# A six-stage fp32 network on one core: the state-space stage reordered, and constant TensorE products put into waits

## The chip, the core and the metric

One NeuronCore of a Trainium2 chip runs the whole program in one launch. The metric is the device time of that launch in microseconds (us). TensorE (PE) multiplies, VectorE (DVE), ScalarE (ACT) and GpSimd (POOL) do the elementwise work, and SyncE's queue (SP) issues most of the transfers.

## What is computed

2048 tokens of width 128 pass through six blocks with residual connections, all in fp32. Cut to what matters here:

```python
x = x + 0.5 * ffn(layernorm(x))     # F, run 0: two layers of local attention (8 heads, window 64) and gated MLP
x = x + ssm(layernorm(x))           # S
x = x + 0.5 * ffn(layernorm(x))     # F, run 1: the same weights
x = x + 0.5 * moe(layernorm(x))     # M, moe 0: 8 experts, the best 2 of each token
x = x + unit(layernorm(x))          # U: gated unit (its Toeplitz part acts on a sequence of length 1)
x = x + 0.5 * moe(layernorm(x))     # M, moe 1

def ssm(x):                         # state size N = 64 for each of the 128 channels
    u = layernorm(x) * gamma + beta             # so x is normalised twice in a row
    h[t] = exp(-exp(log_A) * dt) * h[t-1] + B * dt * u[t]
    y[t] = sum_n C[n] * h[t, n] + D * u[t]
    return y @ W_out.T + b_out
```

## The kernel before, in words

X lies in SBUF as 128 channels (partitions) by 2048 tokens, worked on in four chunks c of 512 tokens. Every engine has its own hand-written program and runs it strictly in order; engines meet at semaphores. So the order written down for each engine is the schedule, and a wait at the head of one engine's program holds all that stands behind it.

**The state-space stage** (plan letter S; line numbers are those of the profile). Each chunk is normalised twice; p = 0 and p = 1 name the two passes. One pass is: `ssm_centred(c, p)` on PE (L526, a product with the centring matrix into bank `SN_CEN[c]`), `ssm_square` on ACT (L1154), `ssm_variance` on PE (L532, a product with the averaging matrix into bank `SN_VAR`), `ssm_root` on ACT (L1163 Ln, L1166 Exp), `ssm_normed` on DVE (L1599 for p = 0, L1602 and L1604 for p = 1). The order of the eight passes is the list `SN_ORDER`; squares, logs and roots have two buffers, used in turn. Then `ssm_transpose(c)` (PE, L540) turns the chunk into 64-token blocks, and `ssm_input(c)` copies the halves out on ACT (L1170) and DVE (L1608). When all four chunks are there, PE forms the block states: 128 products of 64x64 weights with 31 columns (L924, 256 matmul instructions), in four groups of 32, one PSUM bank each. Behind each group DVE runs two scans over the blocks (L1912). Meanwhile ACT takes eight exponentials over the output decays (`decays_exp`, L1183) and POOL multiplies each by C·B (L2172, counted by `gt_done`). PE then forms the outputs in four groups (L936, 256 instructions, each group waits for two more scans; before the first, all eight `gt_done`), transposes them (L945), multiplies by W_out (L956), and DVE adds into X (L1926). `base(c)` (DVE, L1888) adds the bias and the once-normalised value into X; only L1926 needs it. `state_decays(1, .)` (ACT, L1177) are two exponentials that L924 needs.

The stage's first passes are woven into the end of F, run 0, where the last MLP chunk (L777 to L790, `mlp_output(7)`) and the last residual (`mlp_residual`, DVE L1788 and L1793, which counts `x_ffn`) run.

**F, run 1** begins with the first norm (L549, L553, DVE L1627), then steps s of attention: two projections (L602), square sums on PE (L659), scores (L634), and so on.

**M** sends token rows to DRAM by expert: PE writes token rows and router scores of a chunk (`token_rows` L576, `route` L570, `rank` L584 and L585), DVE picks the experts (L1654 to L1708), ACT scales the rows (L1213 to L1225), POOL issues eight indirect transfers for each chunk (L2114). DVE then computes the tile map in 24 chained steps (`map_dve`), SP loads the first tiles, and PE runs 39 tiles of 128 rows: a transpose (`take`, L976), the hidden product (L984), the output product (L994). The outputs go to DRAM by POOL (L2121), come back by SP, and `combine` (L1019) adds the two experts of each token; DVE adds them to X (L1931). **U** weaves its norm (L1031, L1037), up products (L1050), ACT's silu (L1514), gates (DVE L2033), down products (L1057) and the routing of moe 1 into one order; `enter(c)` is token_rows and route of a chunk once its `x_unit` is done.

## Time and profile before

| | us |
|---|---|
| median of 3 runs (lowest, highest) | 1125.36 (1124.89, 1128.22) |
| profiled execution, its own time | 1124.78 |
| its span in the trace | 1123.0 |
| PE busy (share of the span) | 978.7 (87%) |
| DVE, ACT, POOL busy | 733.0, 686.3, 524.6 |

The span counts from the first to the last instruction of the trace; the execution's own time is 1.8 us longer. TensorE's clock has two levels, and the profile lists the level granted in each stretch as a share of full speed: 1.00 is 2.4 GHz, 0.50 is 1.2 GHz. Its mean over the span is 0.942.
### The profile page before, as it was taken

What the parts mean: (1) busy time and instruction counts of PE and PEld (TensorE: products, weight loads), DVE (VectorE), ACT (ScalarE), POOL (GpSimd) and SP (SyncE); (2) the same over time, 40 slices, a digit from 0 to 9 for tenths busy, and PEclk for the clock granted to TensorE, in tenths of its full rate; (3) what the DMA queues carried; (4) which work ended last, traced back from release to release, by engine and by line L of the source; (5) the groups of instructions that cost most, each with busy time, mean ns of one, the idle gap of its engine ahead of it and who ended that gap; (6) DMA issues with size and microseconds to landing.
All of it is one profiled execution on the core that took longest, in us unless ns stands there. A gap on an engine that the chain in (4) does not pass through costs nothing.

```text
span 1123.0 us, 26079 instructions
## 1 busy us (share of the span) xinstructions
PE 978.7 (87%) x9072; PEld 628.4 (56%) x9072; DVE 733.0 (65%) x1689; ACT 686.3 (61%) x1329; POOL 524.6 (47%) x392
## 2 busy tenths in 40 slices
PE   4889999999998968789999999999828996856995
PEld 1445555555555347255555555556428994435995
DVE  1678787787877554378777877778674442665442
ACT  3577686686684572577776776684615663834661
POOL 2555466566442515455444544552463550263552
PEclk9899999999999987899999999999968998877998
DMA  5656464364444600355444444443331222012224
GB/s 180 165 152 144 114 162 115 86 143 114 93 98 104 78 1 3 91 118 115 111 99 97 114 105 98 103 110 82 133 112 53 69 75 82 19 49 66 68 68 127
DMA packets 89712, 109.99 MB, mean 98 GB/s; under 512 B 20368, under 2 KB 74384, under 8 KB 88816
## 3 DMA queue, kind: packets, MB, share of 16 engines
q1 hardware_dynamic: 82160, 91.17, 34.2%
q0 software_dynamic: 4544, 9.35, 2.4%
q10 hardware_dynamic: 2880, 7.81, 2.2%
q8 instruction: 75, 1.23, 0.5%
q14 instruction: 53, 0.43, 0.1%
HBM read 62.66 MB, written 12.07 MB: 67 GB/s over the span
## 4 chain that ended last, share of the span: by engine, by line
PE 74%; ACT 8%; DVE 7%; issue 4%; DMA 4%; POOL 1%; SPq 1%; ACTq 0%; DVEq 0%; POOLq 0%
PE banks L602 9%; PE banks L984 7%; PE banks L994 7%; PE banks L690 5%; PE banks L676 5%; PE banks L651 4%; PE banks L634 4%; PE banks L683 4%; PE banks L790 3%; PE banks L746 3%; PE banks L735 3%; PE banks L659 2%; PE banks L610 2%; DMA arena<-arena 2%; PE banks L1019 2%
## 5 line engine op out<-in xcount | busy, mean ns | idle before, releaser
L2142 POOL TENSOR_TENSOR arena<-arena 128x1024 f32<-128x1024 f32 x64 | 150.9, 2357 | 308.6 <-DVE arena L1735 302.4
L2131 POOL TENSOR_TENSOR arena<-arena 128x1024 f32<-128x1024 f32 x64 | 150.8, 2357 | 27.1 <-ACT arena L1244 27.1
L602 PE MATMUL banks<-arena 128*128 128x512 f32 x256 | 138.8, 630 | 7.1 <-DVE arena L1627 5.9
L1236 ACT ACTIVATE arena<-banks,arena 128x512 f32<-128x512 f32 x128 | 80.7, 682 | 102.0 <-PE banks L683 101.5
L2121 POOL DMA_INDIRECT moe_outs<-arena x78 | 80.9, 1037 | 96.2 <-DVE arena L1986 88.6
L1470 ACT ACTIVATE arena<-banks,arena 128x128 f32<-128x128 f32 x312 | 89.0, 369 | 56.3 <-PE banks L984 56.3
L1727 DVE TENSOR_REDUCE arena<-banks 128x4 f32<-128x512 f32 x128 | 82.4, 685 | 56.7 <-PE banks L634 56.6
L2114 POOL DMA_INDIRECT moe_rows<-arena x64 | 63.7, 996 | 87.0 <-DVE arena L1708 66.7
L1735 DVE TENSOR_TENSOR arena<-arena 128x1024 f32<-128x1024 f32 x64 | 77.9, 1218 | 23.4 <-DMA arena<-arena 23.4
L994 PE MATMUL banks<-arena 128*128 x624 | 86.4, 281 | 3.3 <-ACT arena L1470 2.8
L984 PE MATMUL banks<-arena 128*128 128x128 f32 x624 | 86.8, 284 | 0.3 <-issue 0.2
L1244 ACT ACTIVATE arena<-banks,arena 128x512 f32<-128x512 f32 x128 | 80.7, 688 | 7.6 <-DMA arena<-arena 7.2
L1741 DVE TENSOR_TENSOR arena<-banks,arena 128x512 f32<-128x512 f32 x128 | 81.8, 680 | 0.0
L683 PEld LDWEIGHTS banks<-arena 128*128 128x128 f32 x512 | 59.5, 140 | 39.7 <-issue 32.3
L994 PEld LDWEIGHTS banks<-arena 128*128 128x128 f32 x624 | 76.6, 193 | 7.5 <-issue 6.4
L984 PEld LDWEIGHTS banks<-arena 128*128 128x128 f32 x624 | 79.2, 199 | 1.4 <-issue 0.9
L651 PE MATMUL banks<-arena 128*64 128x65 f32 x2048 | 74.8, 225 | 3.6 <-ACT arena L1236 1.4
L1249 ACT ACTIVATE arena<-banks 128x1024 f32<-128x1024 f32 x64 | 65.6, 1025 | 19.8 <-PE banks L602 18.1
L651 PEld LDWEIGHTS banks<-arena 128*64 128x64 f32 x2048 | 65.7, 137 | 17.9 <-issue 17.9
L683 PE MATMUL banks<-arena 128*128 128x128 f32 x512 | 67.2, 272 | 4.7 <-DVE arena L1741 4.7
L602 PEld LDWEIGHTS banks<-arena 128*128 128x128 f32 x256 | 46.1, 201 | 45.0 <-issue 36.6
L634 PE MATMUL banks<-arena 64*64 64x128 f32 x2048 | 67.7, 270 | 1.5 <-DVE arena L1721 1.5
(230 smaller groups left out, 1944.3 us busy)
## 6 DMA issues: line engine op xcount, KB each, us to landing
arena<-arena SPq DMA_DIRECT2D x256, 128.0 KB, 3.7
arena<-rstd SPq DMA_DIRECT2D x128, 256.0 KB, 4.3
arena<-moe_rows SPq DMA_DIRECT2D x78, 64.5 KB
arena<-in_mw SPq DMA_DIRECT2D x2, 2048.0 KB
arena<-moe_outs SPq DMA_DIRECT2D x16, 256.0 KB, 4.9
arena<-in_rot ACTq DMA_DIRECT2D x12, 256.0 KB, 3.3
arena<-in_wa ACTq DMA_DIRECT2D x2, 1026.0 KB, 6.7
arena<-ssm_a SPq DMA_DIRECT2D x4, 512.0 KB, 6.2
```

Source lines behind the costliest of these rows:

```text
L602: mm(bank[k], w_qkv[d][:, w0:w0 + P], (YA, YM)[d][:, c * C:(c + 1) * C], start=True, stop=True).then_inc(proj, 1)
L634: last = mm(bank[3 + e][r0:r0 + WIN, c0:c0 + P].rearrange("p (b n) -> p b n", b=2), QF[p0:p0 + DH, w * WIN:(w + 1) * WIN], keys if w % 2 e ...
L651: last = mm(bank[5 + e][r0:r0 + WIN, t * VW:(t + 1) * VW], PRT[:, e, w * WIN:(w + 1) * WIN], (VS if w % 2 == 0 else V)[:, t, 2 * hp + e, : ...
L683: last = nc.tensor.transpose(bank[3 + e][:, t * P:(t + 1) * P], PR[:, e, t * P:(t + 1) * P], ident)
L984: last = mm(bank[2 + t % 2][:, j * P:(j + 1) * P], W1E[:, t % 2, j * P:(j + 1) * P], XT[:, t % 2], start=True, stop=True)
L994: last = mm(bank[4 + t % 2][:, 0:DM], GT[:, t % 2, j * P:(j + 1) * P], MW2[:, bass.ds(at * MH + j * DM, DM)], start=(j == 0), stop=(j == M ...
L1470: A(GT[:, t % 2, jj], bank[2 + t % 2][:, jj], ACT.Gelu_apprx_tanh, bias=B1E[:, t % 4, j:j + 1]).then_inc(h_gelu, 1)
L1727: nc.vector.tensor_reduce(mx[:, e], by_row(bank[3 + e][:]), AX.X, ALU.max).then_inc(s_max, 1)
L1741: TT(by_row(PR[:, e]), by_row(bank[3 + e][:]), wide(mx[:, e], P), ALU.subtract).then_inc(s_sub, 1)
L2121: nc.gpsimd.indirect_dma_start(out=outs_dram.ap(), out_offset=bass.IndirectOffsetOnAxis(ap=DST[:, t % 4:t % 4 + 1], axis=0), in_=YO[:, t % ...
L2131: nc.gpsimd.tensor_tensor(TA[:, n % 2], RAW, ROTV[:, :, 0, c * C:(c + 1) * C], ALU.mult).then_inc(cos_done, 1)
L2142: nc.gpsimd.tensor_tensor(TA[:, n % 2], TA[:, n % 2], TB, ALU.add).then_inc(rot_sum, 1)
```

## The change

It has two parts. The first reorders the state-space stage: another `SN_ORDER`, chunk 3's products go to bank 0 instead of 3 (so that they need not wait for chunk 0's copies), every second variance goes to bank 5, the lists of PE, ACT and DVE are rewritten, both `state_decays` are taken early, the first two `decays_exp` stand between the last input copies, and each group of L936 waits only for the `gt_done` of its own pieces. The second adds `warm(to, n)`: n products of two constants (averaging matrix by identity, 128 columns) into a PSUM bank whose content nobody reads then. There are 262 of them in all, none inside the attention steps except eight at step 0 of run 1.

```diff
-        SN_ORDER = [(0, 0), (1, 0), (0, 1), (1, 1), (2, 0), (2, 1), (3, 0), (3, 1)]
-        SN_CEN, SN_VAR = (3, 4, 7, 3), 1
+        SN_ORDER = [(0, 0), (1, 0), (0, 1), (2, 0), (3, 0), (1, 1), (2, 1), (3, 1)]
+        SN_CEN, SN_VAR = (3, 4, 7, 0), (1, 1, 1, 5, 1, 5, 1, 5)
...
-                after(pe, sn_log, i - 1)
-                mm(bank[SN_VAR], mean, sq[:, (i - 1) % 2], start=True, stop=True).then_inc(sn_var, 1)
+                after(pe, sn_log, i - 1 if i < 5 else i - 2)
+                mm(bank[SN_VAR[i - 1]], mean, sq[:, (i - 1) % 2], start=True, stop=True).then_inc(sn_var, 1)
...
+            def warm(to, n):
+                for _ in range(n):
+                    mm(bank[to][:, 0:P], mean, ident, start=True, stop=True)
+
+            def warm_map(to, moe):
+                for k in range(1, MAP_STEPS, 3):
+                    pe.wait_ge(map_dve, MAP_STEPS * moe + k)
+                    warm(to, 4)
+                pe.wait_ge(map_dve, MAP_STEPS * (moe + 1))
+                warm(to, (24, 20)[moe])
...
                     project(s, 1)
+                    if s == 0 and run:
+                        warm(6, 8)
...
                     ssm_centred(0, 1)
+                    ssm_centred(2, 0)
                 mlp_output(7, s)
 
             def ssm():                      # PE
+                ssm_variance(0, 1)
+                ssm_variance(2, 0)
+                ssm_centred(3, 0)
                 ssm_centred(1, 1)
-                ssm_centred(2, 0)
-                ssm_variance(0, 1)
+                ssm_variance(3, 0)
                 ssm_variance(1, 1)
+                ssm_centred(2, 1)
+                ssm_centred(3, 1)
                 ssm_transpose(0)
-                ssm_variance(2, 0)
+                ssm_variance(2, 1)
+                ssm_variance(3, 1)
                 ssm_transpose(1)
-                ssm_centred(2, 1)
-                pe.wait_ge(u_evac, 1)
-                pe.wait_ge(u_evac_dve, 1)
-                ssm_centred(3, 0)
-                ssm_variance(2, 1)
-                ssm_variance(3, 0)
+                warm(2, 3)
                 ssm_transpose(2)
-                ssm_centred(3, 1)
-                ssm_variance(3, 1)
+                warm(2, 4)
                 ssm_transpose(3)
+                warm(2, 6)
...
-                pe.wait_ge(gt_done, 8)
                 for k in range(DM // 4):
                     if k % 8 == 0:
+                        pe.wait_ge(gt_done, 2 + k // 4)
                         pe.wait_ge(state_scan, 2 + k // 4)
...
                 if moe == 0:                # mixture, PE
+                    warm(5, 7)
                     rank(0, 2)
+                    warm(5, 17)
                     pe.wait_ge(x_ffn, NCH + 4)
                     token_rows(0, 3)
                     route(0, 3)
+                    warm(5, 6)
                     rank(0, 3)
+                    warm_map(5, 0)
+                else:
+                    warm_map(2, 1)
...
+                warm(3, 30)                 # behind the last expert tile of each mixture
...
                 rank(1, 0)                  # unit, PE
+                warm(2, 13)
                 enter(1)
...
                 rank(1, 2)
+                warm(2, 12)
                 enter(3)
+                warm(2, 8)
                 rank(1, 3)
...
                     first_variance(norm0, 0)
+                    if run:
+                        warm(6, 10)
...
             def ssm():                      # ACT, the order after the change
+                ssm_square(2, 0), state_decays(1, (0, 1)), ssm_root(0, 1), ssm_root(2, 0), ssm_square(3, 0),
+                ssm_square(1, 1), ssm_root(3, 0), ssm_root(1, 1), ssm_square(2, 1), ssm_square(3, 1), ssm_input(0),
+                ssm_root(2, 1), ssm_input(1), ssm_root(3, 1), decays_exp(0), ssm_input(2), decays_exp(1), ssm_input(3),
+                decays_exp(2) to decays_exp(7)
...
                                             # DVE, the order after the change
+                ssm_normed(0, 1), ssm_normed(2, 0), base(0), base(1), ssm_normed(3, 0), ssm_normed(1, 1), ssm_input(0),
+                base(2), base(3), ssm_normed(2, 1), ssm_normed(3, 1), ssm_input(1), ssm_input(2),
+                dve.wait_ge(u_evac, 3), dve.wait_ge(u_evac_dve, 3), memset of the state banks' first columns, ssm_input(3)
```

The ACT and DVE lists are written here one after another on a line; before, they stood in the order of the old `SN_ORDER`, with `base(3)` behind `ssm_input(3)`, the two `state_decays` behind `ssm_root(3, 0)` and `ssm_root(3, 1)`, and all `decays_exp` behind `ssm_input(3)`.

## Rows read from the trace of the kernel before

**Rows 1.** Windows of PE at half clock: length, PE busy (instructions), clock, DMA, GB/s.
```profile
414.60:435.08 20.48, 16.80 (x368) 0.50 0.01 2
452.15:455.56 3.41, 2.87 (x4) 0.50 0.00 0
...
820.80:851.50 30.70, 10.99 (x48) 0.50 0.23 66
930.00:940.20 10.20, 4.14 (x19) 0.50 0.69 192
971.00:981.20 10.20, 8.32 (x22) 0.50 0.14 45
998.30:1025.60 27.30, 8.77 (x40) 0.50 0.23 68
1104.10:1114.30 10.20, 4.26 (x20) 0.50 0.72 200
```
**Rows 2.** Chain of waits through the state-space stage: start, us, what.
```profile
415.30 13.87 PE banks L924 x256
429.17 2.97 issue
432.14 5.21 PE banks L936 x255
...
438.55 3.70 PE banks L945 x128
```
**Rows 3.** Timeline of POOL, ACT and DVE beside it.
```profile
416.35 15.69 POOL L2172 TENSOR_TENSOR arena<-arena 64x1024 f32<-64x1024 f32 x8 [24.13 <-ACT arena L1183]
415.12 9.37 ACT L1183 ACTIVATE arena<-arena 64x1024 f32<-64x1024 f32 x8
429.21 2.47 DVE L1912 TENSOR_TENSOR_SCAN arena<-arena,banks 64x512 f32<-64x512 f32 x2 [0.95 <-PE banks L924]
```
**Rows 4.** Chain and DVE timeline: the last residual of F, and chunk 3's second pass.
```profile
392.07 0.69 DVE L1793 SCALAR_TENSOR_TENSOR arena<-arena 128x512 f32<-128x512 f32 x1
...
407.53 1.14 PE banks L526 x2
...
411.98 0.70 DVE arena L1602
...
413.31 1.17 PE banks L540 x32
```
**Rows 5.** Weight loads of 64x64 at half (L924) and full clock (L540): ns, min/median/max.
```profile
L924 PEld LDWEIGHTS banks<-arena x256: 175/223/228, 415.3 to 428.8; 64*64 64x64 f32 x128
L540 PEld LDWEIGHTS banks<-arena x128: 129/135/135, 395.9 to 414.2; 64*64 64x64 f32 x128
```
**Rows 6.** PE timeline at the start of F, run 1.
```profile
452.69 3.39 PE L602 MATMUL banks<-arena 128*128 128x512 f32 x4 [2.96 <-DVE arena L1627]
```
**Rows 7.** PE timeline at the end of F and the start of M, moe 0.
```profile
817.28 0.30 PE L584 MATMUL banks<-arena 128*128 128x32 f32 x2
...
821.93 2.07 PE L576 MATMUL banks<-arena 128*128 128x128 f32 x8 [4.12 <-DVE arena L1793]
...
845.07 1.01 PE L976 MATMUL banks<-arena 128*128 128x128 f32 x2 [16.61 <-DMA arena<-moe_rows]
...
851.56 1.06 PE L984 MATMUL banks<-arena 128*128 128x128 f32 x8
```
**Rows 8.** POOL timeline: first indirect transfer of chunk 2 (moe 0) and chunk 3 (moe 1).
```profile
820.54 0.96 POOL L2114 DMA_INDIRECT moe_rows<-arena  x1 [1.60 <-ACT arena L1225]
...
1007.15 0.95 POOL L2114 DMA_INDIRECT moe_rows<-arena  x1 [0.69 <-ACT arena L1225]
```
**Rows 9.** PE timeline: the closing combine; ACT timeline: the fourth silu of U's chunk 2.
```profile
1110.04 9.45 PE L1019 MATMUL banks<-arena 128*128 128x128 f32 x64 [7.45 <-DMA arena<-moe_outs]
...
982.91 0.69 ACT L1514 ACTIVATE arena<-banks,arena 128x512 f32<-128x512 f32 x1 [0.62 <-PE banks L1050]
```
**Rows 10.** PE timeline in U: the entry of chunk 1.
```profile
972.88 2.08 PE L576 MATMUL banks<-arena 128*128 128x128 f32 x8 [3.92 <-DVE arena L2043]
```

More of the change, by code:

```diff
@@ L1162, in ssm_root @@
                     act.wait_ge(unit_done, STEPS)
-                A(lt[:, b], bank[SN_VAR][:], ACT.Ln, bias=eps_c).then_inc(sn_log, 1)
+                A(lt[:, b], bank[SN_VAR[i - 1]][:], ACT.Ln, bias=eps_c).then_inc(sn_log, 1)
                 act.wait_ge(sn_log, i)
@@ L1422, in ssm @@
             def ssm():
+                ssm_square(2, 0)
+                state_decays(1, (0, 1))
+                ssm_root(0, 1)
+                ssm_root(2, 0)
+                ssm_square(3, 0)
                 ssm_square(1, 1)
-                ssm_root(0, 1)
-                ssm_square(2, 0)
+                ssm_root(3, 0)
                 ssm_root(1, 1)
+                ssm_square(2, 1)
+                ssm_square(3, 1)
                 ssm_input(0)
-                ssm_root(2, 0)
+                ssm_root(2, 1)
                 ssm_input(1)
-                ssm_square(2, 1)
-                ssm_square(3, 0)
-                ssm_root(2, 1)
-                ssm_root(3, 0)
-                state_decays(1, (0,))
+                ssm_root(3, 1)
+                decays_exp(0)
                 ssm_input(2)
-                ssm_square(3, 1)
-                ssm_root(3, 1)
-                state_decays(1, (1,))
+                decays_exp(1)
                 ssm_input(3)
-                for q in range(2):
-                    decays_exp(q)
                 for q in range(2, 8):
@@ L1890, in ssm @@
                 ssm_normed(0, 1)
+                ssm_normed(2, 0)
+                base(0)
+                base(1)
+                ssm_normed(3, 0)
                 ssm_normed(1, 1)
                 ssm_input(0)
-                ssm_normed(2, 0)
+                base(2)
+                base(3)
+                ssm_normed(2, 1)
+                ssm_normed(3, 1)
                 ssm_input(1)
-                base(0)
-                base(1)
-                ssm_normed(2, 1)
-                ssm_normed(3, 0)
                 ssm_input(2)
-                base(2)
-                ssm_normed(3, 1)
                 dve.wait_ge(u_evac, 3)
+                dve.wait_ge(u_evac_dve, 3)
                 nc.vector.memset(banks[:, 4 * C:8 * C].rearrange("p (d c) -> p d c", c=NL)[:, :, 0:1], 0.0).then_inc(state_zero, 1)
                 ssm_input(3)
-                base(3)
                 dve.wait_ge(a64_done, 2)
```

## The prediction

> **What bounds the kernel now.** I read the page's clock line first, which dips in the middle and in the last third, then PE by stretches of granted clock, then the chain of waits, and last the timelines around each place where the diff puts something. The windows put ends to the dips [rows 1]: outside the first run of F, where the change does nothing, there are nine low stretches. Seven have a row here; the two of 3.41 us that begin at 458.98 and 465.80 repeat the one at 452.15, with PE busy throughout. Every one begins after PE has stood idle and ends after it has worked again. What is lost is not the stretch but half of PE's busy time in it, and only where PE is on the chain.
>
> The chain of waits through the state-space stage is the other half [rows 2]: 13.87 us of L924, 2.97 us in which PE waits, 5.21 us of L936, then L945. The 2.97 us end with POOL: its eight decay products run from 416.35 to 432.04, one each 1.96 us, and the first L936 asks for all eight [rows 3]. They could not start earlier, since ACT's exponentials stand behind its last input copy and begin at 415.12 [rows 3]. DVE's last pair of scans ends at 431.68, nearly together with them. So L924, the scans and POOL all start from one event, chunk 3's transpose at 413.31.
>
> **Part one: the order of the state-space stage.** In a pass, PE's product to DVE's normalising takes 411.98 - 407.53 = 4.45 us, normalising to transpose 1.33, transpose to the first L924 1.99 [rows 4]. In the first pass the product follows one DVE instruction of 0.70, so 0.75. Chunk 3 can start when the last residual ends at 392.76 [rows 4], so alone it would need 4.45 + 0.75 + 4.45 + 1.33 + 1.99 = 12.97 us, to 405.7; before it took until 415.30, because its first product stood behind chunk 0's copies. The new lists don't reach 405.7, since ACT has to serve all chunks:
> - `ssm_centred(2, 0)` ahead of `mlp_output(7)` is one 512-column product, at most 0.86 us, and fills an idle stretch in part: the residual ends 0.55 later, at 393.3. Both `state_decays` (2.46 us on ACT) lie before `ssm_root(0, 1)`, in the time in which PE does that output. No transfer is moved; their data was asked for long before.
> - From there I walked the three lists with the intervals of that chain, 0.6 for a square or a copy and 1.44 for a root. ACT is nearly without gaps: root(3, 0) at 396.7, root(1, 1) 398.1, two squares, input(0) 401.0, root(2, 1) 402.0, root(3, 1) 404.4 to 405.85. DVE's normed(3, 1) ends at 407.2, chunk 3's transpose runs from 407.2, the last copy ends at 409.5. The six constants behind the transpose (1.4 us) end at 409.6 too. **L924 starts at 409.65, 5.65 us earlier.** The four `base` (0.7 each) lie in DVE gaps while ACT makes roots; without that cover they would cost up to 2.8 us.
> - `decays_exp(0)` now ends at 407.0, and POOL runs from 407.1 for 8 x 1.96, to **422.8** instead of 432.04. Its own part is cheap; the wait by groups lets three groups of L936 finish before that.
> - Scans: the first group of L924 plus 4 x 2.5. At low clock a group takes 13.87 / 4 = 3.47 us and PE paces them (last end 426.0, as before 16.4 us after the start). At full clock a group lies between 1.73 (exactly half) and 3.47 (no gain); the 64-column loads take 223 ns at half and 135 at full [rows 5], a ratio of 1.65, so I take 2.1: scans end at 421.8, and POOL is last.
> - The last group of L936 then takes 0.75 to 1.3, DVE's copy 1.1. L945 starts between 425.0 (all at full clock) and 428.8 (all at half), against 438.55: 9.8 to 13.5 us.
>
> Which it is depends on the clock. L924 ran 13.87 us in the low stretch without lifting it [rows 1, 2], so I doubt that it holds a high one. I take a fall in the middle of L924: L945 at 426.3, and 0.8 us for L945 and L956 beginning low. **Gain 11.5.** The Trainium skill ("TensorE: Matmul & The Clock Gate", LDWEIGHTS) gives a weight load as its columns over a fixed 1.2 GHz. By that L924, which is nearly all loads, would not speed up at either clock, and the stage would give 9.8. The trace disagrees, with 223 ns against 135.
>
> **Part two: the constants.** Their price is from the closing combine [rows 9]: 32 products of this size took 4.26 us at half clock [rows 1] and 5.19 at full, so 7.32 all at full, 0.23 each; 0.46 at half.
> - F, run 1: ten (2.3) in the 2.96 us before the projections [rows 6], eight (1.8) after, of which ACT's square and copies hide all but 0.1. The three low stretches hold 2.87, 3.41 and 3.40 us of PE work on the chain; half is 4.85. The third lies behind a wait of two microseconds that gets no constants, so I take **3.9**.
> - M, moe 0: `warm(5, 7)` stands ahead of `rank(0, 2)`, which followed the MLP output without a gap at 817.28 [rows 7]. That is 1.6 us on the path: DVE's rank, then the last residual, `token_rows(0, 3)`. Those products and the route then run at full clock, 1.8 less, so DVE comes out even. But POOL's chunk 2 starts at 820.54, after ACT [rows 8]; now it waits for the rank at about 821.3, and its eight transfers push chunk 3 by 0.1. After the 17 (3.9 in 4.12), the 6, and the 32 and 24 of the map (12.9 us in the 16.61 before 845.07) the tiles start high. From 845.07 to 851.56 is 6.49 us; at full clock ACT's table load and first gelu lead and it is 4.3. **Gain 2.0.**
> - The 30 behind the last tile (6.9) fit in 7.45 us of idle [rows 9]. In U the combine is low for 4.14 us [rows 1], PE on the chain: **2.1**. At the end 4.26 us: **2.1**. The returning transfers are issued each 0.76 us, two a chunk, faster than 1.8 us a chunk at full clock.
> - U: 13 (3.0) in 3.92 us of idle [rows 10]; the 12 (2.8) and the 8 (1.8) stand in two like waits, of 3.3 and 2.0 us, before and after the fourth entry. PE worked 8.32 us in the low stretch at 971.00 [rows 1]; half would be 4.2, but ACT's fourth silu, which waited 0.62 for PE [rows 9], then follows the third directly, and ACT bounds: 1.0 on the chain. `enter(3)` saves 1.5 more, but of the 2.5 only 1.35 reach the tiles: POOL is busy with chunk 2, and chunk 3's start at 1007.15 waited only 0.69 us for ACT [rows 8]. **1.35.**
> - The tiles of moe 1 would gain 1.35 by the same reckoning as moe 0, but 52 constants (12.0) stand in a longer wait, which leaves over 3 us idle before the tiles: **1.0**.
>
> Sum: 11.5 + 3.9 + 2.0 + 2.1 + 1.35 + 1.0 + 2.1 = 23.95 us. The sum is made against the profiled execution's 1124.78, which lies 0.6 below the median of 1125.36: 1100.8, and 1101 rounded.
>
> **Rivals.**
> - **All gains arrive.** L924 stays at full clock (13.5), F gives 4.85, moe 1 1.35: 27.2, so 1097.5. For it: the constants keep PE working up to L924. Against: L924 didn't lift the clock. 0.2.
> - **L924 runs at half clock from its start**, scans pace on PE, L945 starts at 428.8, the transposes begin low: 9; F 2.5; 20 in all: 1105. For it: L924's own stretch [rows 1, 2]. 0.22.
> - **The constants don't keep the clock high**, the stretches come back elsewhere, and only the order counts: 9.8 to 13.5, less 1.6 for the seven at 817.28: about 1114. Against: in moe 0 products of the same 128 columns lifted the clock by 851.5. 0.08.
> - **Slower: constants at half clock overrun their waits.** At 0.46 each the 56 of the map of moe 0 plus the seven and 17 before come to 36.8 us in about 21 of waiting, the two times 30 to 13.8 in 7.45 each, the 52 of moe 1 to 23.9 in 16.5, the 33 of U to 15.2 in those 9.2, F's 18 about 3 over. The overrun is 16 + 13 + 7 + 6 + 3 = 45 us, against 10 from the order: about 1160. It decides from the point where more than a fifth of the constants (10 of 45) run at half clock on the chain. 0.03.
> - **A list of the new order stalls** (the copies wait for a normalising on DVE): 3 to 5 us of the 11.5 gone, 1105. 0.07.
>
> My forecast has 0.4. The range reaches over all but the third and fourth and half a microsecond past the full gain: 1096 to 1109. About 0.3% is what a measurement of this kernel tells from no change, 3.4 us; no case but the fourth comes near it or past it. Faster 0.95, same 0.02, slower 0.03.
>
> **What would show it.** Right: L924 begins near 409.6, POOL's L2172 ends near 422.8, L945 begins near 426; no stretch at half clock from 820 on except short ones before moe 1; the first L984 group of tile 2 some 4.3 us after the first take. Wrong: scans that end after POOL's products (then L924 paces them), L945 later than 429, a rank of chunk 2 that moves POOL's chunk 3 by more than 0.5, or constants whose mean is near twice 115 ns an instruction, ending after the event for which they fill the time.

## The result and the profile after

The changed kernel takes **1112.43 us** (median of 4 runs, 1107.97 to 1113.72) beside 1125.12 us of the kernel before on the same chip (4 runs, 1124.06 to 1128.22): ratio 0.9866, interval 0.9844 to 0.9888. By the medians it is 12.7 us faster; 24 were forecast, and the time lies above the range of 1096 to 1109. (The ratio, here and below, is estimated from all runs and is not the quotient of the medians, which is 0.9887 here; by the ratio the gain is 15 us.) The profiled execution took 1113.30 us, 11.5 below the one before (1124.78), and the traces are compared on that. Line numbers are now those of the changed kernel: L924, L936, L945, L956 have become L940, L952, L961, L972; L1912 is L1940; L2172 is L2200; L602 is L615; L984, L976, L994 are L1006, L998, L1016; L1019 is L1042; the constants are L582.

PE is busy for longer (978.7 us before) and the granted clock, 0.942 before, is 0.979:

```profile
span 1111.5 us, 27130 instructions
...
PE 1026.3 (92%) x9596; PEld 676.1 (61%) x9596; DVE 731.8 (66%) x1689; ACT 686.5 (62%) x1329; POOL 523.8 (47%) x392
...
PEclk9899999999998999999999999999999999999999
```

So the long low stretches of [rows 1] are gone. Behind the residuals of F, run 0, eight short ones of 3.41 us are left; four of them, as windows (columns as in rows 1, with PEld, DVE, ACT and POOL between):

```profile
427.11:430.52 3.41, 3.11 (x60) 3.14 (x64) 0.15 (x1) 0.60 (x1) 3.09 (x3) 0.50 0.02 5
454.42:457.83 3.41, 3.41 (x5) 1.33 (x6) 0.07 (x1) 1.41 (x2) 3.20 (x3) 0.50 0.95 219
939.11:942.52 3.41, 3.41 (x6) 1.22 (x5) 1.48 (x3) 2.97 (x5) 0.00 (x0) 0.50 0.00 0
969.83:973.24 3.41, 3.41 (x5) 1.33 (x4) 1.41 (x2) 1.68 (x3) 2.50 (x4) 0.50 0.13 41
```

They are short, but PE is busy in nearly all of each, where it worked 11 us of the 30.7 before moe 0. The clock falls about as often, eight times for nine. PE worked 63.1 us at half clock in the nine (119.5 us long), and 26.9 in the eight (27.3 us long).

**The state-space stage** came out as the chain of waits and the timelines show here; they answer to [rows 2, 3, 5]. L940 runs 7.65 us where L924 ran 13.87, with loads of 135 ns where it had 223, and POOL's eight products now end last:

```profile
409.29 1.90 POOL arena L2200
...
423.11 1.91 POOL arena L2200
425.06 1.15 PE banks L952 x64
426.23 1.04 DVE arena L1944
427.28 0.14 issue
427.41 5.20 PE banks L961 x128
432.61 3.77 PE banks L972 x64
436.40 0.70 DVE arena L1954
```
```profile
412.02 7.65 PE L940 MATMUL banks<-arena 64*64 64x31 f32 x256
414.19 9.96 DVE L1940 TENSOR_TENSOR_SCAN arena<-arena,banks 64x512 f32<-64x512 f32 x8 [2.66 <-PE banks L940]
```
```profile
L940 PEld LDWEIGHTS banks<-arena x256: 129/135/135, 412.0 to 419.4; 64*64 64x64 f32 x128
```

**F, run 1** starts with a wait of ACT for a transfer that was not seen before, and then PE at half clock (the last two rows):

```profile
451.56 1.27 ACT L1272 ACTIVATE arena<-banks,arena 128x512 f32<-128x512 f32 x2 [1.01 <-DMA arena<-arena]
...
454.27 1.97 PE L553 MATMUL banks<-arena 128*128 128x512 f32 x2 [3.03 <-ACT arena L1159]
...
456.04 2.77 PE L615 MATMUL banks<-arena 128*128 128x512 f32 x4
```

**The seven constants** ahead of `rank(0, 2)` stand in the chain directly (it counts 1.56 us of their 1.72), and in **the combine** PE waits for each of the first two chunks, whose transfers are issued in 6.27 us (answering to [rows 9]):

```profile
806.44 1.72 PE L582 MATMUL banks<-arena 128*128 128x128 f32 x14
808.00 0.31 PE L597 MATMUL banks<-arena 128*128 128x32 f32 x2
...
919.98 6.27 SPq L507 DMA_DIRECT2D arena<-moe_outs  x8
...
924.01 2.05 PE L1042 MATMUL banks<-arena 128*128 128x128 f32 x16 [0.92 <-DMA arena<-moe_outs]
...
927.21 2.05 PE L1042 MATMUL banks<-arena 128*128 128x128 f32 x16 [1.14 <-DMA arena<-moe_outs]
```

The last residual of F, run 0, itself ends 2.15 us later: 0.4 are the product of `ssm_centred(2, 0)`, and I put the other 1.7 down to a low stretch of 6.83 us at 355, in a part that the diff does not touch. By the same events in both traces (after minus before, us) the way from there divides like this:

| stretch | forecast | measured |
|---|---|---|
| state-space stage, to the first addition into X | -11.5, the product's cost taken off | -11.4, likewise (11.8 less 0.4) |
| F, run 1, to the square sums of step 3 | -3.9 | -1.5 |
| F, run 1, from there to the last square sums | 0 | +0.3 |
| end of F, run 1 (with the seven), and M, moe 0, to the last gelu | -2.0 | -1.4 (+1.5, then -2.9) |
| U, combine included, to the first take of moe 1 | -3.45 | +0.5 |
| M, moe 1, to the last gelu | -1.0 | -0.6 |
| closing combine and what follows it | -2.1 | +0.9 |

In the last row 1.15 us are a scatter to DRAM that landed 3.37 us after its issue, against 2.22 before; in five of the fourteen traces with the 249 constants this step is about a microsecond longer, in none of the six without. The combine itself is hardly shorter: from the first issue of its transfers to its last product it is 13.1 us, where it was 13.3 (the issues began at 1106.15, the products of [rows 9] end at 1119.5):

```profile
1094.96 6.17 SPq L507 DMA_DIRECT2D arena<-moe_outs  x8
...
1098.82 9.26 PE L1042 MATMUL banks<-arena 128*128 128x128 f32 x64 [1.88 <-DMA arena<-moe_outs]
```

The three lower rows, 6.55 us of forecast, gave nothing together.

### The profile page after: what moved, and what is told of

It is laid out like the page before. It is cut to its first block, busy times and chain, and to the rows that moved or that the text cites. A ratio compares the mean times of both kernels' runs of the same rounds, so it can differ in the third digit from the quotient of the medians.

```text
span 1111.5 us, 27130 instructions
## 1 busy us (share of the span) xinstructions
PE 1026.3 (92%) x9596; PEld 676.1 (61%) x9596; DVE 731.8 (66%) x1689; ACT 686.5 (62%) x1329; POOL 523.8 (47%) x392
## 4 chain that ended last, share of the span: by engine, by line
PE 71%; ACT 8%; DVE 6%; DMA 5%; issue 5%; POOL 4%; SPq 2%; ACTq 0%; DVEq 0%; POOLq 0%
PE banks L615 9%; PE banks L1016 7%; PE banks L1006 6%; PE banks L703 5%; PE banks L689 5%; PE banks L664 4%; PE banks L647 4%; PE banks L803 4%; PE banks L696 4%; PE banks L759 3%; PE banks L748 3%; POOL moe_rows L2142 3%; PE banks L672 2%; DMA arena<-arena 2%; PE banks L623 2%
## 5 line engine op out<-in xcount | busy, mean ns | idle before, releaser
L615 PE MATMUL banks<-arena 128*128 128x512 f32 x256 | 136.7, 621 | 4.4 <-DVE arena L1654 3.7
L1016 PE MATMUL banks<-arena 128*128 x624 | 86.4, 281 | 4.1 <-ACT arena L1497 3.5
L1006 PE MATMUL banks<-arena 128*128 128x128 f32 x624 | 84.1, 278 | 0.3 <-issue 0.2
L696 PEld LDWEIGHTS banks<-arena 128*128 128x128 f32 x512 | 60.3, 142 | 38.9 <-issue 32.1
L1016 PEld LDWEIGHTS banks<-arena 128*128 128x128 f32 x624 | 76.3, 192 | 8.6 <-issue 7.3
L1006 PEld LDWEIGHTS banks<-arena 128*128 128x128 f32 x624 | 76.6, 193 | 1.4 <-issue 1.3
L696 PE MATMUL banks<-arena 128*128 128x128 f32 x512 | 67.9, 275 | 4.3 <-DVE arena L1768 4.3
L615 PEld LDWEIGHTS banks<-arena 128*128 128x128 f32 x256 | 45.3, 197 | 41.0 <-issue 35.6
L582 PE MATMUL banks<-arena 128*128 128x128 f32 x524 | 65.1, 285 | 5.4 <-DVE arena L1965 5.4
```

Of the source, the lines that this page charges most:

```text
L615: mm(bank[k], w_qkv[d][:, w0:w0 + P], (YA, YM)[d][:, c * C:(c + 1) * C], start=True, stop=True).then_inc(proj, 1)
L696: last = nc.tensor.transpose(bank[3 + e][:, t * P:(t + 1) * P], PR[:, e, t * P:(t + 1) * P], ident)
L1006: last = mm(bank[2 + t % 2][:, j * P:(j + 1) * P], W1E[:, t % 2, j * P:(j + 1) * P], XT[:, t % 2], start=True, stop=True)
L1016: last = mm(bank[4 + t % 2][:, 0:DM], GT[:, t % 2, j * P:(j + 1) * P], MW2[:, bass.ds(at * MH + j * DM, DM)], start=(j == 0), stop=(j == M ...
```

## The experiments

Eighteen kernels were timed (medians of 4 to 6 runs each, e2 of 11, beside 9 to 16 of the kernel before on the same chip; the ratio is to these):

| kernel | median | ratio (95%) |
|---|---|---|
| e1 order alone | 1120.27 | 0.9937 (0.9917, 0.9958) |
| e2 249 constants alone | 1123.04 | 0.9974 (0.9959, 0.9989) |
| e3 changed, without the seven | 1108.61 | 0.982 (0.9802, 0.9839) |
| e4 e3, all gaps filled | 1107.97 | 0.9826 (0.9805, 0.9846) |
| e5 changed, only the stage's 13 constants | 1120.61 | 0.9939 (0.9922, 0.9957) |
| e6 changed, without these 13 | 1114.81 | 0.9894 (0.9868, 0.992) |
| e7 changed, 21 for the seven | 1118.27 | 0.9911 (0.9882, 0.9941) |
| e8 e3, three fills | 1109.92 | 0.9854 (0.9831, 0.9877) |
| e9 before, takes behind | 1118.22 | 0.9928 (0.9905, 0.9951) |
| e10 changed, takes behind | 1102.59 | 0.9785 (0.9758, 0.9811) |
| e11 e5, takes behind | 1107.19 | 0.9825 (0.9798, 0.9853) |
| e12 e8, takes behind | 1101.14 | 0.9765 (0.974, 0.979) |
| e13 e1, takes behind | 1111.37 | 0.985 (0.9825, 0.9874) |
| e14 e2, takes behind | 1113.86 | 0.9889 (0.9866, 0.9913) |
| e15 e3, takes behind | 1099.90 | 0.9773 (0.9747, 0.9799) |
| e16 e12, returning rows on two queues | 1101.59 | 0.9779 (0.9752, 0.9806) |
| e17 changed, read before the take | 1104.46 | 0.9794 (0.9773, 0.9816) |
| e18 changed, again | 1111.45 | 0.9863 (0.984, 0.9886) |

### The two parts alone, and the clock gaps

e1: `warm` returns at once. e2: the old order, with the 249 constants that lie outside the state-space stage. e3:

```diff
-                    warm(5, 7)
                     rank(0, 2)
```

The 13 constants of the stage are in neither e1 nor e2. e4 is e3 with more constants wherever the trace of after had a wait and then a low stretch: 7 before the last group of L952, 4 before the wait for its last copy, 12 at step 1 of F, run 1, more in both tile maps, in U and behind the last tile.

> The changed kernel without any of the 262 constant products; the reordered state-space stage stays. Theory A (the order carries the gain, the constants win little because DMA, POOL and DVE waits take over where PE gets faster): the stage from its first product of chunk 0's second pass to the first product of F, run 1, is 1 to 3 us longer than the 49.0 us of the changed kernel, the rest of the program is as before, and the whole is 1 to 4 us slower than the changed kernel, 1113 to 1117. Theory B (the constants win what the prediction said, 10 us or more, and something else gave it back): 1120 or more, or the order alone wins less than 5 us.

> The kernel before with the 249 constants that stand outside the state-space stage, and its old order. Theory A: 0 to 3 us faster than before, 1122 to 1125, with half or less of the low-clock time of before. Theory B: 8 to 12 us faster, 1113 to 1117.

> The changed kernel without the seven constants ahead of the rank of chunk 2 in moe 0. If they are on the path, DVE's rank comes 1.6 us earlier; POOL's transfers of chunk 2 and 3 come 0.5 to 1.2 us earlier, and the kernel gains 0.5 to 1.2 us (1111.5). If the clock needs them, a low stretch stands there and nothing is won (1112.4 or more).

> The changed kernel without those seven and with constants in the waits that still had none: before the last group of state-space outputs and before their transposes, at step 1 of F run 1, before the tile maps, more after the tile map of moe 1 and after the last tiles, before the third centring in U and after the second rank. Theory A: low stretches after 380 us all but go, and the time falls by only 2 to 5 us, to 1107 to 1110. Rival, that the eight short low stretches left over eat the gain that was predicted: it falls by 8 us or more, to 1104 or less.

Order alone gives 0.63% and the 249 constants alone 0.26%, the whole change 1.34%. That is more than their sum, but neither of the two has the 13 constants of the stage. The chain of e1 shows what is missing: without them L940 (there L939) falls back to half clock and paces the scans (12.64 us against 9.96), as one of my rivals had it.

```profile
411.01 13.86 PE banks L939 x256
424.87 5.09 PE banks L951 x254
```

(e1 came out as its theory B, e2 as its theory A.) Without the seven the last residual of F, run 1, comes 1.5 us earlier in the trace, and POOL's first transfer of chunk 3, which bounds what follows, 0.8; the median gained 3.8 us, where I had 0.5 to 1.2. Filling the gaps seemed to do what it should where it was put (against e3 the first addition into X comes 1.0 us sooner after the last residual, and step 3 of F 0.8 sooner after that), but e18, the changed kernel with no fill, has both intervals about as short as e4 (40.0 and 33.2 us, e4 40.5 and 33.1). The median did not move. In e4's trace the clock fell near the end of attention, with PE busy 9.51 of 10.20 us, and that cost 4.5 us there:

```profile
778.00:788.20 10.20, 9.51 (x39) 6.41 (x35) 3.21 (x14) 2.49 (x3) 5.32 (x6) 0.50 0.10 31
```

The fills are not shown to be the reason. In e7, which has none, the same stretch came at 775.85 and cost 4.5 too, and short ones stand between 769 and 784 us in e2, e11, e12, e18 (the changed kernel again) and in e13, which has no constants at all. Waits of PE of 1.40 and 1.54 us stand ahead of it in e7, and the same two in e8, where the clock stayed high. What decides it is open.

### Which constants, and what the seven cost

e5 keeps only `warm(2, 3)`, `warm(2, 4)`, `warm(2, 6)`; e6 takes only these away; e7 has `warm(5, 21)` for `warm(5, 7)`; e8 is e3 with three of e4's fills (7, 4 and 12).

> The changed kernel with only the 13 constant products of the state-space stage; the other 249 do nothing (their waits stay). Theory A (the state-space stage carries the gain, and it needs the 13 to keep L924 at full clock): the first scan again about 19.3 us after the last residual of F, run 0, all scans within 10.0 us, and a median of 1112 to 1115, close to the changed kernel; the other 249 are then worth about 0 to 2 us. Theory B (the constants matter along the whole kernel, a few tenths to 2 us in each place): 1116 to 1118, and the changed kernel's last 4 to 6 us come from the 249. If L924 still runs at half clock (scans 12.6 us), the full clock there was chance: about 1119.

> The changed kernel without the 13 constant products of the state-space stage; the other 249 stay. Theory A: L924 falls to half clock as with the order alone, the scans take 12.6 us, the stage gives back 4 us of its gain, and the median is 1116 to 1118. Rival (PE stays busy enough in the new order, and the order alone was slow by chance): scans 10.0 us, 1112, the 13 are worth nothing.

> The changed kernel with 21 in place of the 7 constant products ahead of rank(0, 2): 14 more instructions pairs of 0.23 us at full clock, all on the path to the rank. Theory A (their price is the duration of the row, and nothing is given back): the first indirect transfer of chunk 2 and the last residual of F, run 1, come 3.2 us later than in the changed kernel, and the median is 3.2 us higher, 1115.6, as the kernel without the 7 came out about 1.6 or more below. Rival (my forecast: the full clock that they buy evens them out, or POOL's transfers bound the stage so that PE's rank has slack): less than 1 us more.

> The kernel without the 7, with three fills more: 7 constants before the last group of L952, 4 before the wait for the last copy of the state outputs, 12 at step 1 of F, run 1. Theory A (the two low stretches behind them cost 1.2 us before the first addition into X and 1.0 us at step 1, and only these two are on the path): 2.2 us below the kernel without the 7, 1106 to 1107, and the trace shows 7.9 us from the last copy to the first addition in place of 9.2, and 17.6 in place of 18.65 at step 1. Rival (the clock falls elsewhere instead, as it did in the kernel with all gaps filled, and gives it back): 1108 to 1110.

The thirteen do hold the clock: e5's L940 has the loads of 129 to 135 ns and its scans 9.96 us. In e6, without them, the same products (L937 there) begin at full clock and lose it after 2.48 us; they take 11.84 us, the scans 12.18 (windows of e6, columns as above, the clock third from the end):

```profile
409.55:412.03 2.48, 2.48 (x85) 2.48 (x87) 0.31 (x1) 2.43 (x3) 2.40 (x2) 1.00 0.02 7
412.03:421.40 9.37, 9.37 (x182) 9.31 (x182) 6.99 (x6) 4.34 (x4) 8.99 (x6) 0.50 0.01 2
```

e6's median, 1114.8, lies under the 1116 to 1118 that I had. And e5 is as slow as the order alone, though its stage up to the first addition into X is 3.0 us shorter. This fitted neither theory, and the trace pointed elsewhere: from the third tile's gelu to the last its tiles of moe 0 took 77.7 us, against 73.5 before and 73.7 after, at full clock. Listing the time from gelu to gelu of the tiles from the third on gave single tiles of 2.5 to 3.7 us among those of 1.9 to 2.0: 4 of them before, 2 after, 7 in e5, 12 in e2 (whose profiled execution was its slowest, 1129.57), none in e8, whose profiled execution was the fastest so far, 1105.28. e8's median, 1109.9, falls in the range of its rival all the same. e7's median is 5.8 us above the changed kernel's rather than 3.2, with six such tiles in its profile; there the fourteen added constants put POOL's first transfer of chunk 2 off by 3.1 us more than the low stretch does. The long tile looks like this (timeline of e7):

```profile
1024.49 0.14 PEld L998 LDWEIGHTS banks<-arena 128*128 128x128 f32 x1 [0.51 <-DMA arena<-moe_rows]
1024.49 0.33 PE L998 MATMUL banks<-arena 128*128 128x128 f32 x1 [0.32 <-DMA arena<-moe_rows]
...
1025.36 0.97 PEld L1016 LDWEIGHTS banks<-arena 128*128 128x128 f32 x8 [0.73 <-issue]
...
1026.67 0.29 DVE L2014 TENSOR_TENSOR arena<-banks,arena 128x128 f32<-128x128 f32 x1 [1.72 <-PE banks L1016]
```

The row load comes 0.3 us late, PE waits at the take, and the output product of the tile before, which does not need that load, begins another half microsecond late.

### The takes moved

In the tile loop the take for tile t + 2 goes behind the output of tile t - 1, on top of four kernels:

```diff
                         hidden(t, g0 + t)
-                    if t + 2 < NT:
-                        take(t + 2, g0 + t + 2)
                     if t:
                         expert_out(t - 1, g0 + t - 1)
+                    if t + 2 < NT:
+                        take(t + 2, g0 + t + 2)
```

> The kernel before, with take(t + 2) behind expert_out(t - 1) in both mixtures' tile loops, nothing else. The profiled executions so far took 72.0 to 77.7 us for the 39 tiles of a mixture, whatever the clock, with single tiles of 2.8 to 3.6 us among those of 1.9; in the one looked at a late row load holds the take, and with it expert_out on PE. Theory A (the take's place in PE's order passes the late load on): no tile over 2.6 us, 72 us in each mixture, and 0.5 to 2 us less than before. Rival (the stall comes from the load's lateness itself, wherever the take stands, or ACT's copy now comes later and sets the pace): the same single long tiles, or all tiles over 1.95.

> The changed kernel with the takes behind the outputs. Theory A: no long tiles, and the runs scatter by less than the 5 to 10 us of the kernels so far; median 1108 to 1110, some 3 us below the changed kernel, which shows what of the missing gain was lost in the tiles. Rival: as the changed kernel, 1112.

> The kernel with only the 13 constants of the state-space stage, with the takes behind the outputs. It had come out at 1120.6, no better than the order alone at 1120.3, though its stage was 3 us shorter up to the first norm of F, run 1; its tiles took 77.4 and 74.6 us. Theory A (the 3 us were lost to long tiles): 1115 to 1117 and both mixtures near 72 us. Rival (they are given back before the tiles): 1119 to 1121.

> The kernel without the 7, with the three fills and with the takes behind the outputs. Its best execution without the takes moved was 1105.3 with both mixtures at 72 us, its median 1109.9. Theory A: a median of 1104 to 1106, the best of all versions. Rival: 1109 to 1110.

This two-line move is worth 7.9 us to the kernel before (1126.1 on that chip), 9.8 to the changed one (8.9 against e18), 8.8 to e8 and 13.4 to e5. Why e5 had most to gain is open. The 39 tiles of a mixture, from the end of the first tile's gelus to the end of the last's, take 72.1 to 73.5 us where they took 75.7 to 82.0, except one of 75.8 in e11, with the one long tile that the four traces have from the third tile on. All four medians came out below what I had written, e9's most of all (0.5 to 2 us): the common tiles gain too, from medians of 1.93 to 2.00 us in the traces so far to 1.90 to 1.92. With the takes moved, e11 is at 1107.2; the order alone, e13 below, is at 1111.4, so the 13 constants show there, where e5 and e1 are equal.

### The terms again, with steady tiles

All with the takes behind: order alone (e13), 249 constants alone (e14), the changed kernel without the seven (e15). e16 is e12 with the returning rows of the second expert on ACT's queue:

```diff
-                        for k in range(2):
+                        for k in range(1):
...
+                for b in range(4):               # ACT, behind its last tile
+                    act.wait_ge(outs_out[b], uses(b, moe, NT) * 16)
+                for c in range(NCH):
+                    of = outs_dram.ap()[T + c * C:T + (c + 1) * C].rearrange("(t p) n -> p t n", p=P)
+                    act.dma_start(YC[:, 1, c * TILES:(c + 1) * TILES], of).then_inc(outs_in[c], 16)
```

> Order alone (all 262 constants do nothing) with the takes behind the outputs, to be read against 1118.2, the kernel before with the takes behind. Theory A (without constants L924 runs at half clock and the order gives 8.6 us up to the first addition into X, less what the norm and first steps of F give back): 1110 to 1112. Rival (the order gives all, the 13 nothing): 1107, as with the 13.

> The kernel before with the 249 constants outside the state-space stage, takes behind the outputs. Theory A: F's start 1.5, M 0.7, U and the closing combine 1 to 2, together 3 to 5 us: 1113 to 1115. With order and 13 at 1107.2 and everything at 1102.6 the 249 gave 4.6 there; if they add, 1113.6. Rival (they only pay together with the order): 1117 to 1118.

> The changed kernel without the 7 constants ahead of rank(0, 2), takes behind the outputs; to be read against 1102.6. Theory A (their 1.6 us lie on the path of the last residual of F, run 1, which came 1.5 us later with them, and POOL's chunk 3 gives back 0.7): 1101 to 1101.8. Rival, my forecast (evened out): 1102.6. Third: as without the takes moved, 3 us less, 1099.5.

> The best version so far (1101.1: no 7, three fills, takes behind) with the second expert's half of the returning rows issued on ACT's queue instead of SP's. Eight transfers of 256 KB are issued in 6.2 us there, and the combine's first two chunks wait for them. Theory A (the DMA engines bound it, over 90 per cent busy in that stretch): the second chunk's wait stays, under 0.5 us less in all, 1100.6 to 1101.1. Rival (the issue of 0.76 us each bounds it): the first chunk lands 0.8 us earlier, the second's wait of 1.1 us goes, in both combines, 2 to 3 us less, 1098 to 1099.

Against e9's 1118.2: order -6.9, the 249 constants -4.4, order and the 13 constants -11.0, everything -15.6, without the seven -18.3. Order and 249 constants alone sum to 11.2, and the 4.4 us that everything has beyond them are the 13 constants, which neither e13 nor e14 has: on top of the order they gave 4.2 (e13 to e11). So the parts add up, 6.9 + 4.2 + 4.4 = 15.5. What the 13 would give in the old order no run shows. The traces agree: from the last residual to the first addition into X e13 takes 45.5 us and e10 41.6. The seven cost 2.7 us by the medians (3.8 with the takes where they were) and 0.9 by the traces: from the end of the last square sum of F to POOL's first transfer of chunk 3 it is 68.3 us with them (after, e10, e14), 67.4 without (e3, e15), and 68.1 before. The intervals are too wide to tell 0.9 from 2.7. The profiles of e9 and e15 differ by 18.6 us: stage 14.8, F to its last square sums 0.7, from there to the last gelu of moe 0 1.8, combine and U up to POOL's last chunk 2.5, from there to the last gelu of moe 1 1.0, closing combine 0.6, less 2.8 for what lies before the stage.

The medians of e13 and e14 lie in the ranges of their theories A, and e15's nearest the third case.

The two queues brought nothing (1101.59 against 1101.14). The second chunk's wait is gone, but the first chunk's is longer; from the first issue to the end of the second chunk's products it is 8.2 us in e12 and 8.3 in e16:

```profile
919.76 2.05 PE L1047 MATMUL banks<-arena 128*128 128x128 f32 x16 [1.26 <-DMA arena<-moe_outs]
...
922.03 2.05 PE L1047 MATMUL banks<-arena 128*128 128x128 f32 x16 [0.22 <-DMA arena<-moe_outs]
```
```profile
918.54 3.86 PE L1047 MATMUL banks<-arena 128*128 128x128 f32 x32 [1.62 <-DMA arena<-moe_outs]
```

The first chunk begins 4.5 us after the first issue (914.06) where it was 3.8 (915.92). In 2 us slices of that stretch the DMA engines are over 90% busy in both, and from the first issue to the last landing the eight transfers take 9.5 us in e12 and 9.7 in e16: the engines bound it, not the issue.

### Why the long tiles

Between the take and the output PE's program reads the tile's expert number into a register. e17 moves that read alone, e18 is the changed kernel again:

```diff
-                def expert_out(t, g):
-                    at = pe.value_load(TILE_EI[0:1, t:t + 1], min_val=0, max_val=NE - 1)
+                def expert_out(t, g, at):
...
+                    if t:
+                        at = pe.value_load(TILE_EI[0:1, t - 1:t], min_val=0, max_val=NE - 1)
                     if t + 2 < NT:
                         take(t + 2, g0 + t + 2)
                     if t:
-                        expert_out(t - 1, g0 + t - 1)
+                        expert_out(t - 1, g0 + t - 1, at)
```

> The changed kernel with the read of the expert number (value_load) ahead of take(t + 2), the take itself where it was. Theory A (the long tiles are the read, which PE's program reaches only behind the waiting take, and which is then uncovered): the tiles of each mixture near 73 us from the third gelu on, no L1016 behind an issue wait, and 1103 to 1106, near the version with the takes behind. Rival (the late row load itself): long tiles as in the changed kernel, 1110 to 1113.

> The changed kernel once more, beside e17 on the same chip. Expected: 1112.4 within the scatter of its runs so far (1108 to 1114); with e17 at 1103 to 1106 the difference is 6 to 9 us.

7.0 us between the two on one chip, for the place of one register read. The waits in the tiles of moe 0, of e18 and then of e17, say which part it was: the loads are still late now and then, but the output no longer waits behind them. (Columns: engine, line, released by, us in total, times, longest.)

```profile
PEld banks L1016 <- issue: 2.5, 6, 0.8
PEld banks L998 <- DMA arena<-moe_rows: 1.8, 2, 0.9
...
PE banks L1016 <- ACT arena L1497: 1.3, 2, 0.6
```
```profile
PEld banks L998 <- DMA arena<-moe_rows: 0.6, 3, 0.2
PEld banks L1015 <- issue: 0.6, 1, 0.6
```

While PE waits for a load at the take, its program stands still; the read behind it begins only then, and its own time, hidden beside the hidden product otherwise, comes out in the open. That is my reading of the edit and of the "issue" waits, which fall from six to one; the read itself is in no row. The loads of moe 0 were also less late in e17's execution (0.2 us at most, against 0.9), so the trace alone would not decide it; the runs do, e17's lying at 1100.7 to 1107.0 and e18's at 1110.7 to 1114.9. In the two profiles the tiles of both mixtures together take 7.7 us less, and only part of that are the three long tiles of e18: the common ones go from medians of 1.95 and 1.98 us to 1.90 here too. The two remedies are nearly the same size (1104.5 here, 1102.6 with the take moved), and no tile of e17 is above 2.31 us.

## Why the prediction was wrong

Of the 24 us the profiled execution gave 11.5, and the other 12.5 lie mostly in three places: the combines and U (3.9 missing), the closing combine (3.0) and the start of F, run 1 (2.4); 1.7 lie before the stage, 0.6 in M, moe 0, and the rest in M, moe 1, and the middle of F. Part of it is chance, and twenty traces tell which part: six of kernels without the 249 constants (before, e1, e5, e9, e11, e13) and fourteen with them. The kernels of a group differ in other places, but hardly in these stretches. The means of the two groups, us:

| stretch | without | with | forecast |
|---|---|---|---|
| F, run 1: first addition into X to the square sums of step 3 | 34.9 | 33.4 | -3.9 |
| moe 0: POOL's first transfer of chunk 3 to the third tile's gelu | 22.3 | 21.3 | -2.0 |
| first combine: first issue to the end of chunk 1's products | 9.6 | 8.9 | -2.1 |
| U: from there to POOL's first transfer of chunk 3 | 65.2 | 65.1 | -1.35 |
| moe 1: from there to the third tile's gelu | 21.6 | 21.1 | -1.0 |
| closing combine: first issue to the last product | 13.3 | 12.4 | -2.1 |

Every stretch but U's is clearly shorter with the constants, together by 4.7 us where the sum had 12.45. The terms had the right sign and were too large.

- **State-space stage, forecast 11.5: right in size, by two errors that cancel.** The chain was as drawn. Counted from the last residual, L924 was to start after 16.35 us and did after 17.1; POOL was to end after 29.5 and did after 30.1; L945 was to start after 33.0 and did after 32.5. Step wrong: "so I doubt that it holds a high one". L940 held the full clock throughout, and so did all thirteen traces with the 13 constants ahead of it (scans of 9.96 or 9.97 us in each); in the seven without them they took 12.2 to 12.6. Without the 13 the doubt is right: e6's lost the clock in the middle. I read a stretch in which it had failed to *lift* the clock as evidence that it could not *hold* it. What that gained went to L961 (L945 before), which began low behind 1.25 us of waiting and took 5.20 us for 3.70. That is chance in this execution: e18, the same kernel, has nearly the same wait (1.23) and 3.70 us, and of the nine traces with the 13 and no fills four have 5.2 to 5.4 and five 3.7. The ratio of the two clocks for L924 is 13.87 / 7.65 = 1.81, where I took 1.65 from the loads alone. The Trainium skill's rule that I weighed ("TensorE: Matmul & The Clock Gate", LDWEIGHTS: a load's columns over a fixed 1.2 GHz) would have left L940 at 13.9; the trace contradicts it.
- **F, run 1, 3.9: 1.5 came.** Up to step 1 the start gained 2.8, but step 1 gave 1.1 back. Step wrong: "half is 4.85" and the sum from it. The 3.41 us stretches were counted as pure PE work on the chain, while ACT's copy at step 1 waits for the swap transfer (1.01 us); and the third stretch came back shifted. In the shortest traces, those with the fill of step 1 among them, the way to step 3 is 33.0 us, and in e9 with no constants it is 34.0: there is little more to be had.
- **M, moe 0, 2.0: 1.4 came.** The price of the seven was right: the residual came 1.5 us later, and POOL's chunk 3 0.2 later, where I had 0.1. What "DVE comes out even" passed over is that the same evening out is to be had without them: the other constants give 0.6 at that point (e3), and the seven take it and 0.2 more. From the first take to the third tile's hidden products it is 4.8 us (834.37 to 839.18) for 6.49 before; I had 4.3, and the second row load came late.
- **The combines and U, 2.1 + 2.1 + 1.35: nothing after, 1.3 in the means.** Step wrong: "The returning transfers are issued each 0.76 us, two a chunk, faster than 1.8 us a chunk at full clock", from which I took PE's work as what bounds the combine. The transfers do not land as they are issued. After the change chunk 0's two land 3.0 and 3.6 us after their issue, chunk 1's 4.3 and 5.7, the last four 5.0 to 6.4, with the engines full; chunk 1 arrives 1.1 us after PE could take it, and all 64 products of the closing combine take 9.26 us for 9.45 before. I took the interval of issue for the interval of arrival. In U two low stretches hit PE's work on the chain in places that ran at full clock before, behind waits of 2.07 and 2.60 us. Before had the same wait of 2.07 and kept its clock behind it, and in the other traces with constants U is no shorter either, so why its 1.35 us never came is open.
- **What no term held: the expert tiles.** The sum takes them as they were. In fact each mixture lost 3 to 9 us in them against the traces with the takes moved, changing from one execution to the next and from one kernel to the next, and that hid terms of a few microseconds. It is no part of the 12.5 us missing between the two profiled executions, whose tiles, from the third on, take 146.1 us before and 145.9 after. By the medians the change is worth 15.6 us with the takes moved (e9 to e10), not 12.7, and without the seven 18.3; by the ratios 1.4% against 1.3%. So whether the change itself makes the tiles worse or the 2.9 us are scatter, the intervals do not say.
- **The rivals.** That all gains arrive needed L924 at full clock, which came, and everything else, which didn't. "L924 at half clock" is what the order alone does (e1). That constants keep nothing high and only the order counts gave 1114, close to what was measured, for a wrong reason: the clock did stay high. The slower case, constants that overrun their waits, never began: their instructions lie 115 ns apart as estimated.

The range was too narrow because its ends were made from terms that each lean on one profiled execution, with none for the scatter between executions (of the tiles, of L961, of the stretch at 355), and because six terms each of 1 to 4 us were all taken at nearly their full size. In F and in the combines the removed low stretch exposed a second limit (a transfer, ACT, the next wait), and that is the term that they lacked.

## What to carry to other kernels

Halving half-clock work on the chain is worth only what lies between it and the next wait: before counting half of a stretch, find the transfer or engine that is ready last there, and by when it lands, not when it is issued. Filler products pay where they stand in a true wait and carry a high clock into long work on the chain (13 of them were worth 4 us here, once the tiles were steady), and cost time where the engine had no wait (7 cost 0.9 us by the traces, 2.7 by the medians). One profiled execution does not price a term of 1 or 2 us: nearly the same wait (1.25 and 1.23 us before L961) ended at half clock in one execution and at full in the next. In an in-order engine's loop, keep register reads, and work that needs no load, ahead of a wait for a load: that move, found while looking for something else, was worth 7 to 10 us (13 in e5), near the whole change, and the best version has both (e15, 1099.90 us, ratio 0.9773, interval 0.9747 to 0.9799; e12 and e16 lie within its scatter).

## What the runs showed of the hardware

- The 64x64 loads ahead of 31 columns take 129 to 135 ns at full clock and 223 at half. A run of 256 such instructions, with PE busy throughout, never raised a low clock in 13.87 us (before, e1). It held the full clock for its 7.65 us in all thirteen traces with 13 constants in the waits ahead of it, and without them, in e6, lost it after 2.48 us.
- A wait of 0.3 us for a transfer became more than a microsecond of a tile, by my reading because a register read behind it on PE's program lost its cover (the "issue" of 0.5 to 0.8 us before L1016); tiles of 1.9 to 2.0 us became 2.5 to 3.7. With the read moved ahead of the wait none was above 2.31.
- Eight transfers of 256 KB in rows of 512 B are bound by the DMA engines: from the first issue to the last landing they take 9.5 us when issued on one queue (e12) and 9.7 in pairs on two (e16).
- In seven of the twenty traces the clock fell near the end of attention, between 769 and 784 us, for 3.4 to 10.2 us, in kernels with and without constants (e13 has none) and in one execution of the changed kernel (e18) but not in the other.
